# Two parts of the scaled attention output put next to each other on VectorE, ahead of the last row maximum of each unit

## The reference, cut to what matters

```python
q, k, v, kp = (heads(x @ W.T) for W in (W_Q, W_K, W_V, W_K_prime))
attn   = softmax(q @ k.T  / sqrt(16));  out_std = attn   @ v
attn_p = softmax(q @ kp.T / sqrt(16));  out_p   = attn_p @ v
out = alpha * out_std + (1.0 - alpha) * out_p
h = h + merge_heads(out) @ W_O.T
```

## Time and profile before

| what | value |
|---|---|
| median of 3 runs | 3952.14 us (3947.62 to 3953.11) |
| the profiled execution | 3942.6 us, its span 3940.7 us |
| the stage of this change (`section_duo` with its layer norm and tail) | about 3150 to 3735 us of the span |
| iterations 2 to 29, in which a scaling and a row maximum meet | about 3235 to 3673 us |
| granted TensorE clock, mean over the span | 0.929 |

### The profile page before, as it was taken

How to read it: one execution, slowest core, us unless ns; L and a number is a source line. 1 busy time by engine, 2 the same in 40 slices (tenths; PEclk the granted TensorE clock), 3 DMA queues, 4 the chain that set the end, 5 groups by cost and what they waited for, 6 DMA issues and landing times. The chain is left out here.

```text
span 3940.7 us, 61249 instructions
## 1 busy us (share of the span) xinstructions
PE 3307.3 (84%) x20068; PEld 2464.3 (63%) x20068; DVE 2546.4 (65%) x3859; ACT 2033.6 (52%) x4424; POOL 1890.6 (48%) x1639
## 2 busy tenths in 40 slices
PE   1869989989986888888888888988888888888867
PEld 0669866668974666666666666766655655545534
DVE  6431155553127999999999999999997345555431
ACT  0332223341227777787777777777774344444411
POOL 0123200000316988988898898888985000000044
PEclk9979999999998999999999999999999988988855
DMA  3069710003951111111111111111110000000045
GB/s 98 2 225 333 249 50 1 1 23 116 329 200 33 44 36 42 33 44 34 44 46 44 36 44 34 44 33 42 36 44 22 14 1 1 1 1 1 3 132 153
DMA packets 133783, 263.17 MB, mean 67 GB/s; under 512 B 13872, under 2 KB 104360, under 8 KB 122952
## 3 DMA queue, kind: packets, MB, share of 16 engines
q1 hardware_dynamic: 122120, 228.06, 17.5%
q0 software_dynamic: 11328, 30.95, 2.4%
HBM read 232.46 MB, written 26.51 MB: 66 GB/s over the span
## 5 line engine op out<-in xcount | busy, mean ns | idle before, releaser
L2109 POOL TENSOR_TENSOR ssm_hc<-ssm_hs,ssm_cb 128x1024 f32<-128x1024 f32 x512 | 1204.4, 2356 | 176.8 <-PE ssm_py L2223 155.3
L2609 DVE TENSOR_TENSOR_SCAN ssm_hs<-ssm_da,ssm_pb 128x512 f32<-128x512 f32 x1024 | 1221.5, 1207 | 96.4 <-POOL ssm_hc L2109 91.4
L2223 PE MATMUL ssm_py<-ssm_hc,ident 128*128 128x256 f32 x4096 | 1068.4, 384 | 37.9 <-POOL ssm_hc L2109 37.9
L2422 ACT ACTIVATE ssm_da<-ssm_dt,ssm_an 128x255 f32<-128x255 f32 x2048 | 863.7, 498 | 192.5 <-DVE ssm_hs L2609 154.5
L2223 PEld LDWEIGHTS ssm_py<-ssm_hc,ident 128*128 128x128 f32 x4096 | 709.3, 192 | 118.0 <-POOL ssm_hc L2109 46.1
L2590 DVE TENSOR_TENSOR ssm_pb<-ssm_pb,ssm_dtu 128x512 f32<-128x512 f32 x832 | 563.0, 677 | 44.0 <-PE ssm_pb L2210 23.1
L2210 PE MATMUL ssm_pb<-ssm_bst,ssm_eyeb 96*128 96x256 bf16 x1664 | 328.1, 279 | 140.7 <-DVE ssm_hs L2609 122.1
L2210 PEld LDWEIGHTS ssm_pb<-ssm_bst,ssm_eyeb 96*128 96x128 bf16 x1664 | 133.3, 99 | 346.6 <-DVE ssm_hs L2609 248.4
L1758 DVE TENSOR_REDUCE duo_mxr<-duo_pairs 128x4 f32<-128x1024 f32 x128 | 156.7, 1225 | 184.3 <-PE duo_pairs L1496 159.2
L3435 DVE TENSOR_TENSOR moe_hid<-moe_pu,moe_actg 128x512 f32<-128x512 f32 x71 | 49.1, 692 | 348.9 <-PE moe_pu L3078 348.9
L3078 PEld LDWEIGHTS moe_pu<-moe_xt,moe_up 128*128 128x128 f32 x2272 | 266.5, 193 | 6.4 <-ACT moe_xt L3198 3.0
(11 more groups left out here) (587 smaller groups left out, 5477.7 us busy)
## 6 DMA issues: line engine op xcount, KB each, us to landing
moe_up<-in_moe_up SPq DMA_DIRECT2D x72, 1024.0 KB, 5.0
ssm_cb<-ssm_c_dram SPq DMA_DIRECT2D x64, 1024.0 KB, 5.6
moe_down<-in_moe_down SPq DMA_DIRECT2D x72, 512.0 KB, 5.9
sw_wt<-in_sw_w SPq DMA_DIRECT2D x47, 192.5 KB
moe_x_dram<-moe_tok SPq DMA_DIRECT2D x32, 128.0 KB
moe_yg<-moe_y_dram SPq DMA_DIRECT2D x16, 256.0 KB, 3.0
tok_w<-in_wd SPq DMA_DIRECT2D x4, 576.0 KB
out<-h SPq DMA_DIRECT2D x1, 2056.0 KB, 7.1
```

What stands on the lines that cost most here:

```text
L2109: nc.gpsimd.tensor_tensor(hc[:, n % 2, part_], hs[:, n % 2, part_], cb[:, q % 2, part_, :], ALU.mult).then_inc(s["hc_done"], 1)
L2223: ins = nc.tensor.matmul(sums(j), k.ident[:], hc[:, n % 2, st, :], start=False, stop=(q == QN - 1 and st == NQ_ - 1 and j % 2 == 1))
L2422: ins = nc.scalar.activation(da[:, n % 2, 2 * m + o, 1:L], dt2[:, v, j, 1:L], ACT.Exp, scale=a_n[:, d, j, st:st + 1])
L2609: nc.vector.tensor_tensor_scan(two(hs[:, n % 2, 2 * m:2 * m + 2, :]), two(da[:, n % 2, 2 * m:2 * m + 2, :]), two(pb[:, p % 4]), 0.0, ALU.m ...
```

## The change

In VectorE's loop of `section_duo`, `scale_second(u - 2)` moves from behind `row_maxima(u + 2, 1, 1)` to in front of it, directly behind `scale_first(u - 2)`. Nothing is added or taken away.

```diff
@@ -1857,10 +1857,10 @@
                         lower_query(u + 1)
                     if 2 <= u <= U + 1:
                         scale_first(u - 2)
+                    if 2 <= u <= U + 1:
+                        scale_second(u - 2)
                     if row:
                         row_maxima(u + 2, 1, 1)
-                    if 2 <= u <= U + 1:
-                        scale_second(u - 2)
                     if g == 1 and 0 <= i < B:
                         last_query_max(i)
                     if g == 2 and 0 <= i < B:
```

## The result

| | before | after |
|---|---|---|
| median | 3949.88 us (3937.94 to 3953.11, 4 runs) | 3853.82 us (3837.52 to 3858.87, 4 runs) |
| ratio | | 0.9755 (0.9719 to 0.9791) |
| span of the profiled execution | 3940.7 us | 3856.9 us |
| its mean granted clock | 0.929 | 0.938 |

The changed kernel is faster by 96 us, with an interval of about 83 to 111 us. The forecast was 3875 us, and its range ended at 3856. So the direction was right, and the time lies 2 us outside the range.

A forecast was written before the change was run, and what follows sets the result against it. The prediction took one TensorE stall per iteration, behind ScalarE's exponential and copy and VectorE's addition, as the bound. Direct 41.4 us plus clock 36 us off the median of 3952.1 gave 3875 us, range 3856 to 3912.

The forecast's parts named there:

- The bound: In the stage, TensorE waits for ScalarE's exponential, behind its copy, behind VectorE's last addition: 2.51 us even, 2.12 us odd.
- The direct part, 1.48 us an iteration: In iterations 2 to 29 the addition, and so TensorE's restart, comes 1.48 us earlier: 28 x 1.48 = 41.4 us.
- The delay of the row maximum at nothing, with 0.9 us of cover: On VectorE the later row maximum ends by 2.9 us, before TensorE's burst at 3.4 or 3.8 us; costed at nothing.
- The clock's 36 us: Shorter TensorE stalls in the stage bring fewer clock falls: 36 us of the 40.6 us low-clock cost won, bounds 0 and 45.
- the bound of 45 us: Upper bound of the clock gain: all falls go, with those of iteration 29 behind the counted window.
- the 9.5 us by which executions differ: The profiled execution was 9.5 us under the median of runs shown; subtracted from 3866 to give the range's low end, 3856.
- The upper end of the forecast's own part: Both terms with their bounds were to give 3856 to 3895 us, at chance 0.74.
- The clock swinging on at short stalls: Rival: the copy comes 1.48 us earlier but TensorE's clock falls as often as before; 3911 us, chance 0.19.
- The Trainium skill's remark on brief idling: Sign against the clock gain: TensorE's clock can swing when it idles briefly and often between groups of matmuls.
- The clock getting worse with shorter stalls: Rival: a clock fall could follow each stall, 4.75 us more per iteration; 4003 us, chance 0.02.

The follow-up runs named there:

- The second timing: The changed kernel, unaltered, timed once more against the kernel before: 3854.49 against 3946.98 us, ratio 0.9772 (0.9733 to 0.981).
- half the move: Against the kernel before, only the product of set 1 moved ahead of the row maximum, additions left behind it: 27 iterations 440.65 us, ratio 0.9897.

## Why the prediction was right, and where it was wrong

- *The bound.* Right. One wait of TensorE, for the exponential behind the copy behind the addition. Taking the buffer wait away altogether without touching VectorE's order brought 329.3 us, which is the full-clock time less all the stalls.
- *The direct part, 1.48 us an iteration.* Right: 1.47 us in each of the four groups. Iterations 30 and 31, which had the new order already, were the right rows to price it from.
- *The delay of the row maximum at nothing, with 0.9 us of cover.* Right in the changed kernel: all 28 waits of TensorE's burst still ended with the exponential. Where the cover is gone, with three buffers, the iterations are 2.8 us longer.
- *The clock's 36 us: the term that was mis-sized.* Its mechanism was right: filling the stall alone gave 37 us, and the clock over the iterations was 0.99. But the price of the falls, 40.6 us, came from one profiled execution, and that was the cheapest of three. The 27 iterations took 433.7, 443.4 and 437.5 us, against 393.1 at full clock, so the falls cost 40.6, 50.3 and 44.4 us, 45.1 on average. After the change the four groups at full clock make 52.35 us, or 353.4 for 27 iterations, and they took 355.1: 1.7 us are left, for one fall, where 1.6 falls and 4 us were expected. The term measures 45.1 - 1.7 = 43 us, not 36. Even the bound of 45 us, "all go", is under what one of the profiles lost.
- *The step that failed* is the one from this term to the range: "3856 (3952.1 - 41.4 - 45 = 3866, less the 9.5 us by which executions differ)". Besides the 45, the 9.5 us was wrong: it is the distance of one profile from one median, and no measure of how executions differ. Executions of before on one chip lie up to 46 us apart. In the profiles of this study the first addition of the stage ends anywhere from 3233 to 3269 us, after the same instructions, and the last layer takes 212 or 231 us. A difference of two medians of four runs carries such swings too. The best estimate of the effect itself is the stage's: 83 us, and about 3 us behind it (from the 28th addition to the last it took 38.6, 43.8 and 41.2 us before and 37.8 after). That is 86 us. The second timing gave 75 to 105 us, which holds it; the first gave 83 to 111, which also does. The point forecast of 77 was 9 low of that, about half of it from the falls' price. The 10 us from 86 to the 96 of the medians are not traced to anything; that they are chance is argued from the spread of executions and not shown. The miss itself, 2 us, is as small as the step by which the fourth run moved the median of before (3952.1 to 3949.9), so which side of 3856 the time came out on was luck.
- *The upper end of the forecast's own part,* 3895 us, follows from no sum: with the clock term at its bound of 0 it would be 3911.
- *The rivals.* The clock swinging on at short stalls did not happen, neither at 0.9 nor at 1.4 us. The Trainium skill's remark on brief idling ("TensorE: Matmul & The Clock Gate", "A second HAM failure mode: psum-queue depth-cycling") describes the kernel before, with its stalls of 2.1 to 2.5 us, and not the one after. The clock getting worse with shorter stalls I gave 2 in 100. It did not come here. The one profile of half the move has 0.85 at 2.0 us, against 0.87 to 0.89 at 2.3, but it is that kernel's slowest execution, and its six runs together don't bear this out.

## What to carry to other kernels

When an engine stands still once in each iteration, follow its wait back through the engines to a buffer that is reused, and see what stands in front of the release in that engine's order: here 1.2 us of other work cost 1.5 us of every iteration, and a third buffer was worth more than the best order. Price a stall of TensorE twice, by its own length and by what the clock loses behind it, which here was as much again. And take the price of the falls from more than one profile, and the noise of a forecast's range from the layers that are not touched, when the effect is a few per cent of a long program.

## What the runs showed of the hardware that was not expected

- With one stall of TensorE of 1.8 to 2.6 us in each iteration, its clock was halved for a part of what followed (0.85 to 0.89 on average in five profiles), while stalls of 1.2 and 1.6 us at the same place left it at 1.00. A kernel with 168 extra matmuls in that gap ran 37 us faster than one median of before, and 24 us faster than the other.
- The cost of the falls differs between executions of the same kernel by 10 us, while the iterations of kernels with one fall or none repeat within a tenth: 355.10 and 355.08 us, 337.12 and 337.06 us.
- The last layer took 211 to 213 us in nine profiles and 229 to 231 in five, and the same within each of the three groups of kernels run together on one chip.
